# A transformer block with 1024-token attention: queries and keys projected per group of four heads, a residual loaded in quarters, and a rewritten last chain

## The reference, cut to what is computed

```
x: (4, 1024, 256) f32
mod = silu(c) @ wmod -> sa, ca, ga, sb, cb, gb          # per batch; ga, gb kept away from 0
h = layernorm(x) * (1 + ca) + sa
q, k, v = split(h @ qkv_w.T)                            # 16 heads of 16
x = x + ga * (softmax(q k^T / 4) v @ proj_w.T + proj_b)
h = layernorm(x) * (1 + cb) + sb
for each of 8 experts: loss_n = mean((relu(h @ W_enc[n] + b_enc[n]) @ W_dec[n] + b_dec[n] - h)**2)
e = connected_idx[argmin loss]                          # one choice per batch of 1024 tokens
x = x + gb * (h @ W_base + b_base + relu(h @ W_down[e] + b_down[e]) @ W_up[e] + b_up[e])
```

## Time and profile before

| | before |
|---|---|
| runs, us | 1154.0, 1151.95, 1148.45 |
| profiled execution, us | 1148.24 |
| its span, us | 1146.4 |
| mean granted clock of TensorE | 0.947 |
| TensorE / VectorE / ScalarE / GpSimd busy, us | 1064.5 / 814.1 / 644.1 / 127.0 |
| HBM read / written, MB | 15.95 / 4.22 |

### The profile page before, as it was taken

The page is one execution under the profiler, slowest core; times in us unless marked ns, Lnnn a source line. Parts: engine busy times, 40 slices in busy tenths (PEclk is TensorE's granted clock), DMA queues, the critical chain, the costliest instruction groups (busy, mean ns, idle before and its releaser), DMA issues.

```text
span 1146.4 us, 15955 instructions
## 1 busy us (share of the span) xinstructions
PE 1064.5 (93%) x5820; PEld 494.6 (43%) x5820; DVE 814.1 (71%) x1593; ACT 644.1 (56%) x1293; POOL 127.0 (11%) x251
## 2 busy tenths in 40 slices
PE   6997999899989999999989999999989999889966
PEld 3443444233433355445434354445433554333644
DVE  3775888689878877777878878777887767661232
ACT  3143677578666666665666666566666555556310
POOL 3000121000202210000301210000300000210000
PEclk8668899899999999999999999999999999988989
DMA  7503400331132003301332003302440000200001
GB/s 235 90 14 52 67 20 1 56 56 57 24 56 42 20 11 51 58 10 56 70 63 30 17 11 56 57 16 67 73 56 2 1 1 25 74 1 1 1 1 42
DMA packets 31346, 47.03 MB, mean 41 GB/s; under 512 B 6611, under 2 KB 23512, under 8 KB 31260
## 3 DMA queue, kind: packets, MB, share of 16 engines
...
...
q10 hardware_dynamic: 416, 0.07, 0.0%
HBM read 15.95 MB, written 4.22 MB: 18 GB/s over the span
## 4 chain that ended last, share of the span: by engine, by line
PE 77%; DVE 10%; ACT 4%; DMA 3%; SPq 3%; issue 2%; POOL 1%; ACTq 0%; DVEq 0%
PE pX L570 23%; PE pE L570 20%; PE pO L570 20%; PE pM L570 10%; DVE mx L965 5%; DMA QO<-lo 2%; ACT P L843 2%; SPq L1362 1%; DVE lo L1068 1%; ACT hi L893 1%; SPq L1371 1%; DVE X L1104 1%; PE pE L681 0%; PE pE L617 0%; POOL x L1296 0%
## 5 line engine op out<-in xcount | busy, mean ns | idle before, releaser
L965 DVE TENSOR_REDUCE mx<-pM 128x1 f32<-128x512 f32 x1006 | 633.2, 683 | 159.7 <-PE pM L570 157.4
L843 ACT ACTIVATE P<-pE 128x512 f32<-128x512 f32 x1024 | 545.6, 598 | 322.7 <-PE pE L570 321.5
L570 PE MATMUL pM<-KO,QO 48*128 48x512 f32 x1006 | 375.4, 465 | 9.0 <-DVE mx L965 5.8
L570 PE MATMUL pE<-QO,KO 50*128 50x512 f32 x1024 | 367.4, 449 | 15.1 <-ACT P L843 7.3
L570 PEld LDWEIGHTS pE<-QO,KO 50*128 50x128 f32 x1024 | 168.8, 191 | 282.3 <-issue 186.1
L570 PE MATMUL pO<-P,V 128*17 128x512 f32 x2048 | 268.9, 627 | 0.0
L570 PEld LDWEIGHTS pM<-KO,QO 48*128 48x128 f32 x1006 | 167.5, 193 | 41.0 <-DVE mx L965 32.1
L570 PEld LDWEIGHTS pO<-P,V 128*17 128x17 f32 x2048 | 43.0, 98 | 116.1 <-issue 116.1
L570 PE MATMUL pX<-h1T,wqkv_s 128*128 128x512 f32 x116 | 65.8, 673 | 14.5 <-DVE lo L1068 14.5
L1268 POOL CAST mh<-mxc 128x16 fp32r<-128x16 f32 x32 | 6.8, 214 | 518.1 <-DVE mxc L974 518.1
L570 PE MATMUL pX<-X,Hb 128*128 128x258 f32 x208 | 54.5, 395 | 2.4 <-DVE lo L1068 1.5
...
## 6 DMA issues: line engine op xcount, KB each, us to landing
...
out<-x SPq DMA_DIRECT2D x16, 256.0 KB, 2.2
...
xin<-in_x SPq DMA_DIRECT2D x12, 256.0 KB, 2.6
QO<-mT SPq DMA_DIRECT2D x128, 4.0 KB
```

Source lines behind the costliest of these rows:

```text
L570: return e.matmul(o, lhsT, rhs, start=start, stop=stop)
L843: e.activation(P[:, u % 3, j, :], bank(s), ACT.Exp).then_inc(*empties(s))
L965: e.tensor_reduce(mx[:, hq % 2, k:k + 1, kh], bank(s), AX.X, ALU.max, negate=True).then_inc(*empties(s))
```

## The change

1. A block of `qk` is now one group of four heads, queries and keys together (64 rows each), `qk(b, g, half)`. The weights' columns are reordered on the host, and the factor 0.25 of the queries comes from a column of `cst`. `KO` and `QO` have a slot for each of four groups. A group's block is due every 16 key steps; its 12 transfers, three in each place, all precede the next block.
2. At the start, the first group's blocks go in token halves, keys issued by GpSimd and queries by SP.
3. `x2` comes in four loads (`xload`), each after the store of the same quarter of the batch before, and the bias is added per quarter (`addx`); `wpg` and `wbg` have steps and semaphores of their own (`prep`, `prepb`).
4. The last batch takes all four first halves of queries first.
5. The chain after the last score tile is written out by hand, and the last `mid` writes into `nbe`, so that both halves have their own buffer. `SHARE` rises from 1.45 to 1.6.

```diff
-SHARE = 1.45
+SHARE = 1.6
...
-SEQ += [(4 * NB - 4 + g, c) for g, c in ((0, 0), (1, 0), (0, 1), (2, 0), (3, 0), (1, 1), (2, 1), (3, 1))]
+SEQ += [(4 * NB - 4 + g, c) for c in range(2) for g in range(4)]
...
+    for gi in range(2, 4 * NB):
+        u = {2: 0, 3: 8, 14: 177, 15: 188}.get(gi, 16 * gi - 36)
+        at(u, ("qk", gi // 4, gi % 4, 0), ("qk", gi // 4, gi % 4, 1))
...
-            halves = ((B - 31, (0, 1)), (B, (2, 3))) if q == LAST else ((B + 3, (0, 1, 2, 3)),)
+            halves = ((B - 30, (0, 1)), (B, (2, 3))) if q == LAST else ((B + 3, (0, 1, 2, 3)),)
...
-            if b:
-                at(B + 0, ("qk", b, 1, 0, 0), ("qk", b, 1, 0, 1))
-                at(B + (4 if b == LAST else 6), ("qk", b, 1, 1, 0), ("qk", b, 1, 1, 1))
...
-            at(B + (36 if b == LAST else 60), ("prep", b))
+            u = B + (20 if b == LAST else 53)
+            at(u, ("prep", b))
+            for k in range(4):
+                at(u, ("xload", b, k))
+                at(u + 6, ("addx", b, k))
+            at(u + 2, ("prepb", b))
...
-            at(B + 33, ("qk", b + 1, 0, 0, 0), ("qk", b + 1, 0, 0, 1))
-            at(B + 38, ("qk", b + 1, 0, 1, 0), ("qk", b + 1, 0, 1, 1))
...
     if kind == "prep":
-        return [(("out", b - 1, 3), 1)] if b else []
+        return [(("mid", b - 1, 0), 0)] if b else []
+    if kind == "prepb":
+        return [(("prep", b), 1)] + ([(("out", b - 1, 3), 1)] if b else [])
+    if kind == "xload":
+        return [(("out", b - 1, a[0]), 1)] if b else []
+    if kind == "addx":
+        return [(("prep", b), 1), (("xload", b, a[0]), 2)]
     if kind == "proj":
-        return [(("atturn", b, a[0] // 2 + i), 0) for i in (0, 2)] + [(("prep", b), 4)]
+        return [(("atturn", b, a[0] // 2 + i), 0) for i in (0, 2)] + [(("addx", b, a[0]), 1)]
...
-            for _ in range(3 if u0 >= UB * LAST else 2):
+            for _ in range(3):
                 if moving:
                     out.append(moving.popleft())
...
-                    later = m < NM and ready(u) < 2
+                    later = m < NM and ready(u) < (1 if u0 >= UB * LAST else 2)
...
+    now(("oturn", NU // 8 - 1))
+    fill(len(spare) > 4)
+    now(("atturn", q, 1), ("atturn", q, 3))
+    fill(len(spare) > 4)
+    for k in (2, 3):
+        now(("proj", q, k), ("bn2", q, k), ("ln2s", q, k))
+    now(("ln2n", q, 2), ("ln2n", q, 3))
+    fill(len(spare) - 2)
+    now(("xturn", q, 2), ("xturn", q, 3), ("xsq", q, 2), ("xsq", q, 3), *(("enc", q, t) for t in range(4, 8)))
+    now(*(("half", q, p, 1) for p in range(4)), ("pick", q), ("select", q), ("fetch", q))
+    fill(len(spare))
+    now(("mid", q, 0), ("mid", q, 1), *(("out", q, k) for k in range(4)))
...
-                    e.activation(halves(oc, w, b)[0][:, cs], bank(s), ACT.Copy,
-                                 scale=1.0 if w else 0.25).then_inc(s_hi, 1)
+                    e.activation(halves(gi)[0][:, cs], bank(s), ACT.Identity, scale=qscale).then_inc(s_hi, 1)
...
                 elif kind == "mid" and last:
                     b, h = s[1:]
-                    if (b, h) != (0, 0):
+                    if (b, h) == (LAST, 1):
+                        act.wait_ge(s_zero, 3)
+                    elif (b, h) != (0, 0):
...
+                elif kind == "addx":
+                    b, k = s[1:]
+                    pool.wait_ge(d_x2[k], 16 * (b + 1))
                     pool.wait_ge(*link.now())
-                    pool.wait_ge(d_x2, 16 * (b + 1))
-                    for t in range(8):
+                    for t in (2 * k, 2 * k + 1):
                         a = e.tensor_tensor(x2[:, t, :], x2[:, t, :], bc[:, 0, :], ALU.add)
                     a.then_inc(s_x2, 1)
...
+                elif kind == "copy" and s[1]:
+                    gi, w, i = s[1:]
+                    sp.wait_ge(*emptied("qk", gi // 4, gi % 4, 0))
+                    sp.wait_ge(*emptied("qk", gi // 4, gi % 4, 1))
+                    sp.wait_ge(d_kone, 64)
+                    if gi >= 4:
+
+                        sp.wait_ge(*full("E", 8 * SEQ.index((gi - 4, 1)) + 7, 3))
+                    e.dma_start(*move(gi, w, i, thirds(gi, w))).then_inc(landed(gi)[0], 16)
...
+                elif kind == "xload":
+                    b, k = s[1:]
                     if b:
-                        sp.wait_ge(d_out, 64 * b)
+                        sp.wait_ge(d_out[k], 16 * b)
                     else:
-                        sp.wait_ge(*full("ln1turn", 0, 3))
-                    e.dma_start(x2[:, :, :], x_tiles[b]).then_inc(d_x2, 16)
+                        sp.wait_ge(*full("ln1turn", 0, k))
+                    e.dma_start(x2[:, 2 * k:2 * k + 2, :], x_tiles[b, :, 2 * k:2 * k + 2, :]).then_inc(d_x2[k], 16)
```

231 lines of the change are left out of this document (120 added, 111 removed).

## The result

The kernel before ran 9 times, median 1152.78 us (1148.45 to 1159.32), the changed one 9 times, median 1141.5 (1137.01 to 1143.91). The ratio is 0.9892, 95% interval 0.9866 to 0.9918: 11.3 us faster by the medians. The sum had 31.5 us, and the measured median lies above the top of the range, 1138.

The account below looks back on a forecast made before the run. TensorE, busy 93% of the span, was taken as the bound through its stalls and half clock. Terms 15 + 10.5 + 2 + 7 - 3 = 31.5 us off the profiled 1148.2 gave a forecast of 1117 us, range 1100 to 1138.

Parts of the forecast that it names:

- E: The start: first group's transfers begin some 5 us sooner, but TensorE's unchanged work sets the first maximum; 0 us (-1 to 2).
- A: Query and key projections: spacing blocks removes TensorE's waits for `lo` and half clock behind them; 15 us (4 to 22).
- F: What is added: quarter loads 0, column scale 0, VectorE work bunched by `SHARE` 1.6 -3 us (-8 to 0).
- the exception at group 14: Near key step 177: group 14 waits behind group 13's last transfer, 3.8 us, with half clock 6.5 in all.
- rivals 4 and 5: Quarter loads of the residual: 4, late maxima transfers, 1179 us, chance 0.05; 5, fixed cost of three more loads, 1143, 0.03.
- B: Last batch's preparation on GpSimd: divided and earlier, it removes TensorE's 7.37 us wait and half clock; 10.5 us (0 to 11).
- D: The chain after the last score tile: reordered steps and second buffer give 10.2, less 3.1 for Gram pieces; net 7 us.
- C: Last batch's first token half: its chain begins eight key steps sooner; net 2 us (-4 to 8).
- Rival 3: VectorE takes over: removed stalls return as waits for maxima, no more than D is won; 1141 to 1150 us, chance 0.06.

Follow-up runs that it names:

- e1: The changed kernel with all four transposes of the first batch's normalised tokens ahead of the first projection again: 1135.47 us.
- e5: The kernel before with only the written last chain and the second hidden buffer: 1140.84 us.
- e15: The kernel before with the last batch's preparation due at key step 236 instead of 228, plus a GpSimd wait ahead of `fetch`: 1136.07 us.
- e16: The kernel before with `SHARE` 1.6 instead of 1.45, plus a GpSimd wait ahead of `fetch`: 1144.29 us.
- e17: The kernel before with the new last chain, preparation due at 236, `SHARE` 1.6 and a GpSimd wait ahead of `fetch`: 1117.19 us.
- e6: The kernel before with its blocks of eight heads set farther apart in all batches, plus a GpSimd wait ahead of `fetch`: 1151.23 us.
- e9: The kernel before with blocks set apart in the first three batches only, plus a GpSimd wait ahead of `fetch`: 1143.06 us.
- e18: The kernel before with new last chain, preparation due at 236, `SHARE` 1.6, first three batches' blocks set apart, GpSimd wait ahead of `fetch`: 1111.57 us.
- e4: The changed kernel with `SHARE` 1.45 again: 1134.73 us.
- e7: The changed kernel with the first layer norm turned first and groups 14 and 15 due at key steps 183 and 191: 1127.66 us.
- e8: The changed kernel with all four mends (start, groups 14 and 15 later, `SHARE` 1.45, constants of 0.5 as scales): 1118.82 us.
- e10: The changed kernel with start mended, groups 14 and 15 later and `SHARE` 1.45, the column of constants kept as scale: 1127.56 us.
- e14: The changed kernel with start mended, groups 14 and 15 later, `SHARE` 1.45, column scale kept, last batch's preparation late and in one piece: 1121.47 us.
- e13: The changed kernel with start mended, groups 14 and 15 later and constants of 0.5 as scales, `SHARE` staying 1.6: 1126.24 us.
- e11: The changed kernel with all four mends, but the last batch's halves in the order of the kernel before: 1123.07 us.

## Why the prediction was wrong

The sum was 31.5 us and 11.3 came. Two steps failed most: E, put at nothing, and A with F, put at 12. Term by term:

**E, the start, "that work is unchanged: 0".** This step failed. The work is unchanged but its order is not: the new list puts a projection ahead of two turns, and TensorE waits inside its own pass. 7.2 us in the trace, 6.0 us by e1. The listing of the order showed it; the prediction looked at the transfers and not at TensorE's own row of steps.

**A, projections, "I take 15".** This step failed in size, and by more than E. The waits for `lo` fell by 9.1 us, as forecast (9.2), and the exception at group 14 was priced rightly: 3.8 and 2.3 us, where the wait has 3.77 and mending it takes 6.6 us off key steps 176 to 192. But all of this was taken as time won, with 0.7 us deducted for VectorE, the engine that the prediction itself named as next. Waits for maxima rose by 7.0 us. From the first exponential to key step 232 TensorE stands idle 38.7 us instead of 41.3, and the stretch is 5.9 us longer, with 8.5 us more of TensorE's work in it. So A and F together gave some 3 us in these two executions (estimate, from those two numbers), where 12 were forecast. Waits for maxima stand at 5.5 to 5.8 us in the five kernels with the old blocks in the old places (before, e5, e15, e16, e17), at 8.0 to 10.6 in the three with these blocks set apart (e6, e9, e18), and at 11.1 to 14.5 in all twelve with blocks of four heads (the change, e1 to e4, e7, e8, e10 to e14), at either share. That they go with the placing of blocks is shown by this; which of VectorE's steps each such wait stands behind was not tried, nor what the blocks of four heads give alone.

**F, the share, "-3", and the scale, I take 0.** The share's mechanism is refuted: neither in the kernel before nor in the change does 1.6 raise the waits for maxima (5.7 against 5.8 us, 12.8 against 14.5). Nor does TensorE wait longer for the steps ahead of the second layer norm (`x`, 0.9 us in the change, 3.2 in e4). Its price in the change is not settled. In the kernel before 1.6 is 9.0 us faster, with an interval clear of no change. In the change it is 6.8 us slower (e4), in the mended change 0.1 us either way (e7, e10), with the constants as scale 7.4 us slower (e13, e8); all of these intervals overlap. A loss of 3 us is thus neither confirmed nor excluded. The Trainium skill, "ScalarE: Activation LUTs", section "What ACT_TABLE_LOAD costs", says that each operand given as a column adds about 93 ns to an activation; the trace agrees, 687 against 597 ns. That this is lost "in the 44% that ScalarE is idle" was wrong: these 28 instructions stand in front of a `lo` for which TensorE waits, and 2 us of waits are measured. The quarter loads show no cost on TensorE, though no run has them alone: GpSimd stood 10.6 us for them instead of 1.3, but no wait of TensorE for moved maxima is in the list of waits. So rivals 4 and 5 are out. With them goes the estimate of 24 us by the Trainium skill, "DMA: Bandwidth & Descriptors", section "Anatomy of one DMA", which gives its 2.0 us for transfers issued by GpSimd, while these are SP's.

**B, preparation, "10.5".** Right in place, too high in size for this version: key steps 232 to 240 take 6.8 us less. The wait for `mhl` is gone, but waits for maxima of 0.89 and 1.94 us stand near the same place, and 6.8 us at 0.50 with them. The reason was only half right. Not the dividing but the order on GpSimd's queue does it: e15 takes the same wait away with the piece undivided, and there these key steps take 11.1 us less, near the 10.5. The rest of its 17.2 us is known by the medians alone.

**D, the last chain, "Sum 10.2" and "-3.1. Net 7".** The 10.2 are in the trace (65.7 to 55.4), and e5 has 12.4 in its chain and 13.0 in its time. The deduction of 3.1 us for Gram pieces moved ahead is not seen. e5 leaves all of them in the chain and it is 12.4 us shorter all the same; the change has 42 of these 106 matmuls ahead, and key steps 240 to 255 are shorter, not longer. Why they cost nothing there was not tried. Too low by 3 to 6.

**C, first token half, "2".** Key steps 240 to 255 are 4.5 us shorter in the change, but with and without the new order of halves they take 58.7 and 59.0 us (e8, e11). Not told apart from nothing.

So where did the gain go? 35.1 us is what the change gives once its start, group 14, share and scale are mended. The change as it stood lost 22.7 us of this: 6.0 at the start and 4.2 at group 14 measured alone, and the rest when share and scale are mended on top. Of that rest only the 2 us of waits for `lo` have a place in the trace; the remainder is known by its time alone. The 35.1 look close to the sum of 31.5, but that sum already held the stall at group 14 (6.1) and the 3 of the share, so for the mended version the prediction's own terms give 40.6. That the two come near each other is luck in part, A being too high while D was too low. D and B alone gave 13.0 and 17.2 us in the kernel before; if they gave as much in the mended change, which is not shown, 4.9 us would be left for A, C and F, where the prediction had 14. Rival 3, VectorE taking over, had the measured median in its band (1141 to 1150); its mechanism had a share (7.0 us more of waits for maxima) but was not the whole, since D came in full and the start was elsewhere.
